# Attention scores on 32-row tiles in four row groups, and every eighth rectification on ScalarE

## The reference

```python
xn = layernorm(x)
# attention: 8 heads, 2 query/key dims and 16 value dims a head
scores = einsum('bmhd,bnhd->bhmn', q, k) / sqrt(2)
scores = where(scores >= 0, scores, 0.2 * scores)      # leaky rectifier
out = einsum('bhmn,bnhd->bmhd', softmax(scores), v)
attn = gamma * out + xn
# ffn: 16 experts (12 MLPs), top 2 of each token, capacity 1024
y = x + attn + ffn(xn)
```

## Time and profile before

| | |
|---|---|
| time, median of 3 runs | 941.46 us (941.45 to 942.2) |
| span of the profiled execution, first to last instruction | 940.0 us |
| TensorE busy | 861.2 us, 92% |
| VectorE busy | 735.3 us, 78% |
| ScalarE busy | 691.3 us, 74% |
| GpSimd busy | 601.5 us, 64% |
| mean granted TensorE clock | 0.981 of full speed |

### The profile page before, as it was taken

One profiled execution on the slowest core, in us unless ns is written; L12 is line 12 of the kernel. 1 busy time (PEld: TensorE's weight loads), 2 busy tenths in 40 slices (PEclk: granted clock), 3 DMA queues, 4 the chain that ended last, 5 costly groups with the idle time before them and its releaser, 6 DMA issues. The chain is left out here.

```text
span 940.0 us, 20061 instructions
## 1 busy us (share of the span) xinstructions
PE 861.2 (92%) x7499; PEld 348.9 (37%) x7500; DVE 735.3 (78%) x859; ACT 691.3 (74%) x811; POOL 601.5 (64%) x610
## 2 busy tenths in 40 slices
PE   0688269999999999999999999999999999999997
PEld 0444112222222224776867732222222222222222
DVE  5788889999999994101011099999999999999996
ACT  0578888888888887444453568888888888888886
POOL 3355247777777663999999226657567575765782
PEclk9999659999999999999999999999999999999999
DMA  7833101111111112233242210102112111210202
GB/s 214 303 66 74 32 27 33 51 40 51 47 27 36 25 38 88 90 121 116 93 138 71 94 44 22 40 19 59 36 25 59 25 36 29 70 29 13 69 18 55
DMA packets 71225, 59.36 MB, mean 63 GB/s; under 512 B 33770, under 2 KB 58178, under 8 KB 71136
## 3 DMA queue, kind: packets, MB, share of 16 engines
q1 hardware_dynamic: 61520, 48.06, 17.6%
q0 software_dynamic: 8192, 9.37, 3.6%
q10 hardware_dynamic: 1424, 0.76, 0.3%
HBM read 31.58 MB, written 30.02 MB: 66 GB/s over the span
## 5 line engine op out<-in xcount | busy, mean ns | idle before, releaser
L1133 DVE TENSOR_SCALAR ps<-ps 128x1024 f32<-128x1024 f32 x512 | 600.1, 1224 | 14.6 <-PE ps L825 11.7
L718 ACT ACTIVATE pr<-ps 128x1024 f32<-128x1024 f32 x512 | 523.4, 1023 | 104.5 <-PE ps L835 72.9
L855 PE MATMUL ps<-pr,vp 128*32 128x256 f32 x4096 | 327.2, 392 | 0.1
L835 PE MATMUL ps<-q,kz 64*128 64x512 bf16 x1024 | 200.7, 389 | 10.2 <-DVE ps L1133 4.4
L825 PE MATMUL ps<-q,kz 62*128 62x512 bf16 x1024 | 200.3, 389 | 2.9 <-DMA q<-parts_dram 1.3
L505 POOL DMA_INDIRECT xs<-eout,idxs x128 | 129.0, 1008 | 105.0 <-ACT pr L718 75.5
L490 POOL DMA_INDIRECT disp<-xn,idx x128 | 125.9, 984 | 50.8 <-issue 29.2
L835 PEld LDWEIGHTS ps<-q,kz 64*128 64x128 bf16 x1024 | 49.0, 93 | 225.7 <-DVE ps L1133 188.4
L1152 DVE TENSOR_TENSOR pr<-ps,parts 128x1024 f32<-128x1024 f32 x12 | 14.7, 1225 | 149.6 <-PE ps L920 149.6
L855 PEld LDWEIGHTS ps<-pr,vp 128*32 128x32 f32 x4096 | 81.1, 108 | 119.4 <-issue 117.6
L744 ACT ACTIVATE pr<-ps,b1s 128x512 f32<-128x512 f32 x96 | 65.8, 687 | 53.7 <-PE ps L909 53.7
(11 more groups left out here) (122 smaller groups left out, 530.3 us busy)
## 6 DMA issues: line engine op xcount, KB each, us to landing
moved<-att SPq DMA_DIRECT2D x480, 8.0 KB
disp<-pr SPq DMA_DIRECT2D x12, 512.0 KB, 4.9
eout<-pr SPq DMA_DIRECT2D x12, 512.0 KB, 2.9
y<-in_x SPq DMA_DIRECT2D x8, 512.0 KB, 8.1
out<-y SPq DMA_DIRECT2D x7, 512.0 KB
w<-in_w1t SPq DMA_DIRECT2D x12, 256.0 KB, 3.2
w<-in_w2t SPq DMA_DIRECT2D x12, 256.0 KB, 3.4
xs<-disp SPq DMA_DIRECT2D x6, 512.0 KB, 4.9
```

The source lines that it names most:

```text
L718: act.activation(pr[:, c % BUFS, 2 * pair:2 * pair + 2, :], ring[i % RING], ACT.Exp, scale=SLOPE).then_inc(S["exps"], 1)
L835: last = pe.matmul(ring[i % RING][:, k, :], kz[r:r + TILE, hg, pair, kc * P:(kc + 1) * P], q2[r:r + TILE, hg, qh * HALF:(qh + 1) * HALF], ...
L855: last = pe.matmul(acc[p % 2][32 * g:32 * g + 32, cols], vp[:, hg, kc, g, :], pr[:, c % BUFS, g % PAIRS * 2 + g // PAIRS, cols], start=(kc ...
L1133: dve.tensor_scalar(s, s, 0.0, 1.0 / SLOPE - 1.0, ALU.max, ALU.mult).then_inc(S["relu"], 1)
```

## The change

- TILE becomes 32. One head takes one row tile: 18 rows of products, zeros, and the shift in row 31 (ONES). q2 gets an index for the pair, as kz has it, and is twice as large.
- Both operands are held twice (SETS = 2): in rows 0 to 63 and in rows 64 to 127. A unit of an even key block uses the tiles at rows 0 and 32, one of an odd key block those at 64 and 96. Units i and i + 2 lie in neighbouring key blocks, and so in different halves of the array.
- load_operands still issues 12 DMAs, each for two heads. The small DMAs that write -1 into kz become 16, from 8.
- Units with i % 8 == 6 are rectified by ScalarE, ahead of the exponential of unit i - 1, with a semaphore of their own (relu_act). VectorE leaves them out, and shifted waits for the one or the other.

```diff
-TILE = 64
-ONES = TILE - 2
+TILE = 32
+ONES = TILE - 1
+SETS = 2
+SHARE, MINE = 8, 6
-        q2 = sb("q2", [P, NHG, M], BF16)
+        q2 = sb("q2", [P, NHG, PAIRS, M], BF16)
+        def by_scalar(i):
+            return i % SHARE == MINE
+        def rectified(i):
+            mine = (i + SHARE - MINE) // SHARE
+            return ("relu_act", mine) if by_scalar(i) else ("relu", i + 1 - mine)
+        def rows_of(z, k):
+            return TILE * (2 * z + k)
...
-            for hg in range(NHG):
-                for g in range(HG):
-                    r = TILE * (g // PAIRS) + ONES + g % PAIRS
-                    sp.dma_start(kz[r:r + 1, hg, g % PAIRS, :], rowones[:]).then_inc(S["kz_init"], 16)
+            for z in range(SETS):
+                for k in range(2):
+                    r = rows_of(z, k) + ONES
+                    for hg in range(NHG):
+                        for pair in range(PAIRS):
+                            sp.dma_start(kz[r:r + 1, hg, pair, :], rowones[:]).then_inc(S["kz_init"], 16)
...  (in load_operands)
+                for k in range(2):
+                    heads = slice(hg * HG + k * PAIRS, hg * HG + (k + 1) * PAIRS)
+                    krows = parts_dram[1, :, tok].rearrange("(r h) t -> r h t", h=H)[:, heads, :]
+                    qrows = parts_dram[0, :, tok].rearrange("(r h) t -> r h t", h=H)[:, heads, :]
+                    for z in range(SETS):
+                        r = rows_of(z, k)
+                        sp.dma_start(kz[r:r + NPROD, hg, :, :], krows[0:NPROD]).then_inc(S[f"ld{hg}"], 16)
+                        sp.dma_start(q2[r:r + NPROD, hg, :, :], qrows[0:NPROD]).then_inc(S[f"ld{hg}"], 16)
+                        sp.dma_start(q2[r + ONES:r + TILE, hg, :, :], qrows[NPROD:NROW]).then_inc(S[f"ld{hg}"], 16)
...  (ScalarE)
+            def rectify(i):
+                act.wait_ge(S["s1"], i + 1)
+                s = ring[i % RING]
+                act.activation(s, s, ACT.Relu, scale=1.0 / SLOPE - 1.0).then_inc(S["relu_act"], 1)
...
+                    if by_scalar(i + 1) and i + 1 < end:
+                        rectify(i + 1)
                     exponentials(i)
...  (TensorE; scores, and shifted with TILE for ONES)
-                    r = TILE * k
+                    r = rows_of(kc % SETS, k)
-                                     q2[r:r + ONES, hg, qh * HALF:(qh + 1) * HALF], start=True, stop=True,
+                                     q2[r:r + ONES, hg, pair, qh * HALF:(qh + 1) * HALF], start=True, stop=True,
...  (shifted)
-                pe.wait_ge(S["relu"], i + 1)
+                name, count = rectified(i)
+                pe.wait_ge(S[name], count)
...  (VectorE, in rectify)
+                if by_scalar(i):
+                    return
```

More of the change, by code:

```diff
@@ L202, in build @@
                  "qz_init weighted at_rdy sum_rdy inv_rdy row_step route ones_rdy max_rdy off_rdy reset_rdy r_exp cnt_rdy pos_rdy ztile init_rdy kz_init "
-                 "ld0 ld1 vp_rdy s1 relu s2 exps pv acc_evac o_rdy turned rg_rdy att_rdy spread0 spread1 y_att "
+                 "ld0 ld1 vp_rdy s1 relu relu_act s2 exps pv acc_evac o_rdy turned rg_rdy att_rdy spread0 spread1 y_att "
                  "scat staged pool_step carry "
@@ L298, in _ @@
                 sp.wait_ge(S[f"shift_out{u}"], 16 * B)
-            sp.wait_ge(S["kz_init"], 16 * NHG * HG)
+            sp.wait_ge(S["kz_init"], 16 * NHG * SETS * HG)
             def load_operands(b, hg):
@@ L304, in load_operands @@
                     sp.wait_ge(S["s2"], UP * (pass_at(b - 1, hg, NQ - 1) + 1))
[L305 to L314, removed]
+                tok = bass.ts(b, M)
+                for k in range(2):
[7 more added lines that the diff above has]
+                        sp.dma_start(q2[r + ONES:r + TILE, hg, :, :], qrows[NPROD:NROW]).then_inc(S[f"ld{hg}"], 16)
             def store_sequence(s):
@@ L396, in _ @@
             pool.memset(kz[:].rearrange("p a e m -> p (a e m)").bitcast(F32), 0.0)
-            pool.memset(q2[:].rearrange("p a m -> p (a m)").bitcast(F32), 0.0).then_inc(S["qz_init"], 1)
+            pool.memset(q2[:].rearrange("p a e m -> p (a e m)").bitcast(F32), 0.0).then_inc(S["qz_init"], 1)
             def prologue(at):
@@ L831, in shifted @@
                 p, hg, qh, kc, pair = unit_of(i)
-                pe.wait_ge(S["relu"], i + 1)
+                name, count = rectified(i)
+                pe.wait_ge(S[name], count)
                 for k in range(2):
-                    r = TILE * k
+                    r = rows_of(kc % SETS, k)
                     last = pe.matmul(ring[i % RING][:, k, :], kz[r:r + TILE, hg, pair, kc * P:(kc + 1) * P],
-                                     q2[r:r + TILE, hg, qh * HALF:(qh + 1) * HALF], start=False, stop=True,
+                                     q2[r:r + TILE, hg, pair, qh * HALF:(qh + 1) * HALF], start=False, stop=True,
                                      tile_position=(r, 0), skip_group_check=True)
```

## The result

| | before | after |
|---|---|---|
| time, median | 941.83 us | 965.22 us |
| ratio, 95% interval | | 1.0247 (1.0231 to 1.0262) |
| span of the profiled execution | 940.0 | 963.5 |

A forecast was written before the change was run, and what follows sets the result against it. It took a 2.40 us loop over TensorE and ScalarE, not VectorE, as the bound. 940.0 + 1.5 (profile to median) + 24.3 (moved rectifications) - 6.9 (transpose) + 4 (set-up) = 963 us, +2.3%; range 940 to 984.

The forecast's parts named there:

- The sum: Whole kernel: 24.3 us for moved rectifications, -6.9 for the hidden transpose, +4 for set-up, giving 963 us.
- The loop of 2.40 us: Attention: shifted product, exponential, next score product, values, next shifted product; from unit i to i+2 in 2.40 us.
- 16 x 1.20: Attention: a pass of 16 units at 1.20 us each, 19.20 us, without the 0.23 of transpose and reciprocal.
- The row tiles: Attention products on TensorE: score product starts 0.05 us after the shifted one instead of 0.24; alone worth 0.
- closest spacing: Attention: least time from one chain's shifted product to the other chain's, 0.94 us after the change, 1.13 before.
- Rival 1: Attention: tiles do not overlap across units, so an insertion costs 0.57 us; 975 us in all; chance 0.15.
- The share: Attention, ScalarE: each of 64 moved rectifications makes 2.40 us into 2.78, costing 0.38, 24.3 us in all.
- The transpose: Attention, VectorE, unit 5 of a pass: its 0.23 us hides behind the delayed exponential, 30 times, -6.9 us.
- The set-up: Prologue, SP queue: eight more small loads delay the stores of parts and so the third cast; +4 us.
- Rivals 2: Attention: VectorE's busy share is real and sets the pace, so moving work is faster; 911 us, chance 0.11.
- 3: Attention: smaller tiles also shorten the loop, to 2.30 us, if the 0.32 or 0.57 shrinks; 942 us, chance 0.13.
- 4: Attention, ScalarE: Relu and Exp exchange tables, 64 x 2 loads of 1.28 us; 1126 us, chance 0.03.

The follow-up runs named there:

- e1: The changed kernel with VectorE rectifying every unit again, row tiles and set-up loads kept: 946.94 us, ratio 1.0045 to the kernel before.
- e4: The changed kernel, but in moved units ScalarE rectifies one head and VectorE the other: 946.88 us, ratio 1.0041 to the kernel before.
- e2: The kernel before with its own tiles, plus one unit of eight rectified by ScalarE: 971.11 us, ratio 1.0298.
- e5: The changed kernel with one unit in sixteen moved to ScalarE, unit 6 of each pass: 953.41 us, ratio 1.0126 to the kernel before.
- e6: The changed kernel with one unit in sixteen moved to ScalarE, unit 14 of each pass: 969.37 us, ratio 1.0294 to the kernel before.
- e3: The changed kernel with the rows of -1 in kz written by 4 longer DMAs instead of 16: 960.58 us, ratio 1.0186 to the kernel before.

## Why the prediction was right

*The sum.* The change was forecast to add 21.5 us, and added 23.4. Attention had 24.3 - 6.9 = 17.4 of it and took 17.6; the set-up had 4 and took 5.9.

*The bound.* The loop of 2.40 us, not VectorE's 99.5%, sets the pace. Shown from both sides: with the share VectorE's rectifications take 65.5 us less (534.6 against 600.1) and the stretch is longer; without it the tiles alone change nothing (e1); an insertion that fits in the loop is free (e4); no version went below 16 x 1.20.

*The row tiles: 0.* Right, with 0.02 instead of the 0.05 that I took from one product to the next, and 0.91 instead of 0.94 for the closest spacing. Rival 1 (no overlap across units) is ruled out by the rows of the kernel after, and its arithmetic confirmed by e2, which has that spacing (0.57 worked out, 0.57 in the timeline, 0.59 by the pass).

*The share: 0.38 per moved unit.* The timeline has 2.78 where 2.78 was worked out, from slightly different parts: 0.92, 0.91 and 0.95 for the 0.94, 0.92 and 0.92 of the sum. The unknown price, a Relu in PSUM, is 1.02 long and lets the next exponential start after 0.95: not dearer than on VectorE, where two start 1.13 apart.

*The transpose: -6.9.* Right: it shows at 19.41 a pass without the share and all but 0.04 of it is gone with it (e5: 19.62 for 19.20 + 0.38). What I had not seen is that this hangs on the places of both moved units: moved alone, unit 14 makes the transpose cost 0.52 (e6).

*The set-up: +4; it was +5.9.* The mechanism is the one forecast (e3). That the third cast came at 45.26, for a forecast of 44.9, is in part luck, because two errors cancel. The 16 loads and the fill left the queue at 39.71 instead of 41.05. The four stores then took 3.97 us to issue instead of 2.0, while the DMA engines were full (share 1.02 from 40 to 43); the forecast had carried their issue time over from the kernel before. The term came out too small mainly because it had nothing for TensorE's clock: after the stop the next step took 0.94 us more, so that the third cast was 4.35 late (against 40.91) and the fourth 5.29 (50.04 against 44.75). The remaining 0.6 is within the scatter of the prologue. The operand loads stayed covered, but barely: the first score products start 0.99 ahead of the first rectification (132.08, 133.07), where before they started 3.37 ahead.

*Rivals 2, 3, 4.* No faster pass, no shorter loop (0.32 and 0.57 stand as before), and no table load between L733 and L741.

## What to carry to other kernels

An engine that shows as 99% busy need not be the bound: where its instructions start at a fixed delay after another engine's, it may be waiting. Look for the loop that closes over several engines, and add it up from start to start. Work moved to an idle engine that is part of that loop costs what exceeds its gap there, so its length and its place count, not the sum of the work. And a step put ahead of others on a DMA queue is paid for by whoever waits behind them.

## What the runs showed of the hardware that I had not expected

- After 5.60 us without a product, TensorE's granted clock was 0.64 of full from 46 to 48 us and 0.51 from 48 to 50. A cast that came 4.35 us late left the next one 5.29 late.
- A Relu from PSUM to PSUM and an exponential from PSUM to SBUF take ScalarE the same time (1021 and 1020 ns for 1024 columns).
- One-row loads from SBUF were dear to issue: 16 of them held SP's queue for 11.09 us, 8 for 5.99, and 4 with four times the length for 3.26.
- Four stores that took 2.0 us to issue in the kernel before took 3.97 in the change, in a stretch where the DMA engines were full (share 1.02, 416 GB/s). Whether the full engines are the reason is not shown.
